# New orders of work in the attending stage of a decoder layer

## The reference

```python
x = layernorm(x + mix(x))                      # token mixing by per-head Fourier products and a running sum
q, k, v = heads(x @ W_q + b_q), heads(ctx @ W_k + b_k), heads(ctx @ W_v + b_v)     # 16 heads of 32, 77 keys
scores = where(mask == 0, -1e6, q @ k.T / sqrt(32))
x = layernorm(x + (softmax(scores) @ v) @ W_o + b_o)
x = layernorm(x + x @ quantized(kernel) + bias + (x @ a) @ b)
```

## Time and profile before

| what | us |
|---|---|
| median of 3 runs | 965.15 (964.72 to 967.47) |
| profiled execution, span | 964.6 |
| TensorE busy in it | 917.6 (95%) |
| VectorE, ScalarE, GpSimd busy | 666.7, 376.8, 337.8 |
| mean granted TensorE clock | 0.982 of full speed |
| attending stage in it | from 475.5 to the end |

### The profile page before, as it was taken

The page is one execution under the profiler, slowest core; times in us unless marked ns, Lnnn a source line. Parts: engine busy times, 40 slices in busy tenths (PEclk is TensorE's granted clock), DMA queues, the critical chain, the costliest instruction groups (busy, mean ns, idle before and its releaser), DMA issues.

```text
span 964.6 us, 14638 instructions
## 1 busy us (share of the span) xinstructions
PE 917.6 (95%) x4476; PEld 754.5 (78%) x4476; DVE 666.7 (69%) x1128; ACT 376.8 (39%) x1403; POOL 337.8 (35%) x310
## 2 busy tenths in 40 slices
PE   5898999999999999999779999999999999999987
PEld 4784888888888888888668788888888888888775
DVE  3363466665656565555667888979889798887957
ACT  3152120101010111102287566656567565666610
POOL 2000243232222232324236434444443444433733
PEclk9998999999999999999979999999999999999999
DMA  5944201221203020203423122131222203120021
GB/s 179 326 148 172 90 1 52 80 80 52 104 28 127 3 87 1 88 23 116 134 81 102 25 79 73 40 113 24 89 63 78 75 21 122 30 89 21 17 77 44
DMA packets 72346, 76.02 MB, mean 79 GB/s; under 512 B 38567, under 2 KB 40871, under 8 KB 72303
## 3 DMA queue, kind: packets, MB, share of 16 engines
q1 hardware_dynamic: 72303, 75.49, 24.4%
HBM read 52.60 MB, written 22.87 MB: 78 GB/s over the span
## 4 chain that ended last, share of the span: by engine, by line
PE 41%; DVE 4%; ACT 2%; issue 2%; POOL 2%; POOLq 0%; DVEq 0%
PE shared_ps L74 31%; PE score_ps L74 4%; PE shared_ps L1146 4%; ACT probs L1352 2%; PE shared_ps L1109 1%; PE shared_ps L1179 1%; POOL probs L1501 1%; DVE score_ps L1658 1%; DVE xT_lo L1615 0%; DVE x_and_res L1704 0%; DVE top_s L1663 0%; DVE pT_lo L1642 0%; POOL x_and_res L1516 0%; DVE y L1682 0%; DVE w_o_lo L1825 0%
## 5 line engine op out<-in xcount | busy, mean ns | idle before, releaser
L1352 ACT ACTIVATE probs<-score_ps,top_s 128x77 f32<-128x77 f32 x512 | 159.0, 359 | 36.9 <-DVE top_s L1663 36.9
L1352 ACT ACTIVATION_READ_ACCUMULATOR probs<-score_ps,top_s 128x1 f32 x512 | 122.9, 240 | 0.0
L1501 POOL TENSOR_TENSOR probs<-probs,per_total 128x616 f32<-128x616 f32 x64 | 82.7, 1309 | 65.9 <-DVE per_total L1670 65.7
L1494 POOL TENSOR_TENSOR rstd<-ve,half_power 128x1 f32<-128x1 f32 x64 | 42.4, 662 | 157.1 <-DVE ve L1693 152.5
L722 POOL TENSOR_TENSOR vals<-qs_prod 128x512 f32<-128x512 f32 x32 | 41.1, 1296 | 127.1 <-DVE qs_prod L804 127.1
L713 POOL TENSOR_TENSOR mix_rstd<-mix_ve,half_power 128x1 f32<-128x1 f32 x32 | 22.0, 688 | 175.4 <-DVE mix_ve L823 175.4
L1658 DVE COPY_PREDICATED score_ps<-hidden,masked 128x616 f32<-128x616 int32 x64 | 66.2, 1034 | 11.6 <-PE score_ps L74 11.6
L1359 ACT ACTIVATE pT_hi<-shared_ps 103x512 fp32r<-103x512 f32 (+1 forms) x96 | 54.7, 612 | 46.0 <-PE shared_ps L1146 45.5
L672 ACT ACTIVATE v_sb<-v_ps 128x512 f32<-128x512 f32 x32 | 18.9, 594 | 133.9 <-PE v_ps L74 133.9
L679 ACT ACTIVATE qT_hi<-vals 128x512 fp32r<-128x512 f32 x32 | 19.4, 631 | 122.3 <-POOL vals L722 106.2
L1642 DVE TENSOR_TENSOR pT_lo<-shared_ps,pT_hi 103x512 fp32r<-103x512 f32 (+1 forms) x96 | 64.5, 684 | 0.0
(11 more groups left out here) (218 smaller groups left out, 2660.1 us busy)
## 6 DMA issues: line engine op xcount, KB each, us to landing
x_tok<-in_x SPq DMA_DIRECT2D x8, 1024.0 KB, 5.9
x_res<-in_x SPq DMA_DIRECT2D x8, 1024.0 KB, 8.0
x_between<-mix_x SPq DMA_DIRECT2D x32, 256.0 KB, 2.0
x<-x_between SPq DMA_DIRECT2D x8, 1024.0 KB, 5.5
x_tok<-x_between SPq DMA_DIRECT2D x8, 1024.0 KB, 5.7
out<-y_out SPq DMA_DIRECT2D x32, 256.0 KB, 2.0
wqkv_sb<-in_w_qkv SPq DMA_DIRECT2D x4, 768.0 KB, 7.8
keys_split<-w_q_hi SPq DMA_DIRECT2D x8, 154.0 KB, 5.4
```

The lines of the kernel that those rows point to most:

```text
L1352: nc.scalar.activation(probs[:, t % 2, j * KEYS:(j + 1) * KEYS], score_ps[:, g, k * KEYS:(k + 1) * KEYS], ACT.Exp, bias=top[:, t % 2, j:j ...
L1494: nc.gpsimd.tensor_tensor(rstd[:, n:n + 1], ve[:, n:n + 1], half_power[:], ALU.pow).then_inc(rstd_ready, 1)
L1501: nc.gpsimd.tensor_tensor(p, p, per_total[:, t % 2, h * heads:(h + 1) * heads].unsqueeze(2) .to_broadcast([P, heads, KEYS]), ALU.mult).the ...
```

## The change

All lists of `attend` are written anew: that of the banks in all kinds of step (that of the end only in its line breaks), and those of TensorE, ScalarE, GpSimd and VectorE. The end's list of TensorE stays. No call is added or dropped. The core of the diff, with the bank orders, TensorE's full step and start step, the first part of ScalarE's full step, GpSimd's full step, the first half of VectorE's full step, and the last lines of VectorE's end:

```diff
-BANK_ORDER = ["V0", "V1", "V2", "V3", "O0", "P00", "O1", "P01", "O2", "T0", "P02", "F0", "P10", "P11", "T1",
-              "O3", "X0", "X1", "X2", "F1", "X3", "T2", "P12", "Q0", "F2", "P20", "P21", "Q1", "T3", "Q2",
-              "P22", "F3", "P30", "P31", "P32", "Q3"]
-
-
-START_ORDER = ["P00", "P01", "P02", "X0", "X1", "X2", "X3", "P10", "P11", "P12", "Q0", "P20", "P21", "Q1",
-               "P22", "Q2", "P30", "P31", "P32", "Q3"]
-CLOSING_ORDER = ["V0", "V1", "V2", "V3", "O0", "P00", "O1", "P01", "P02", "T0", "O2", "P10", "P11", "P12",
-                 "F0", "T1", "O3", "P20", "P21", "F1", "T2", "P22", "P30", "F2", "T3", "P31", "P32", "F3"]
-END_ORDER = ["V0", "V1", "V2", "V3", "O0", "O1", "O2", "T0", "O3", "T1", "F0", "T2", "F1", "T3", "F2", "F3"]
+BANK_ORDER = ["V0", "V1", "V2", "V3", "P00", "O0", "P01", "O1", "P02", "T0", "O2", "O3", "P10", "X0",
+              "F0", "P11", "T1", "X1", "X2", "P12", "X3", "F1", "Q0", "T2", "P20", "Q1", "F2", "P21",
+              "T3", "P22", "Q2", "P30", "F3", "P31", "P32", "Q3"]
+
+
+START_ORDER = ["X0", "X1", "X2", "P00", "P01", "X3", "P02", "P10", "P11", "Q0", "P12", "Q1", "P20",
+               "Q2", "P21", "P22", "Q3", "P30", "P31", "P32"]
+CLOSING_ORDER = ["V0", "V1", "V2", "V3", "O0", "P00", "O1", "T0", "P01", "P02", "O2", "F0", "P10",
+                 "T1", "P11", "P12", "O3", "F1", "T2", "P20", "P21", "P22", "F2", "T3", "P30", "P31",
+                 "P32", "F3"]
+END_ORDER = ["V0", "V1", "V2", "V3", "O0", "O1", "O2", "T0", "O3", "T1", "F0", "T2", "F1", "T3", "F2",
+             "F3"]
...
                 score(i, s, 1, 1)
+                turn_probs(i, s, 0, 0)
                 project_o(i, s, 0)
-                turn_probs(i, s, 0, 0)
+                turn_probs(i, s, 0, 1)
                 project_o(i, s, 1)
-                turn_probs(i, s, 0, 1)
+                score(i, s, 2, 0)
+                score(i, s, 2, 1)
+                turn_probs(i, s, 0, 2)
+                turn_x2(i, s, 0)
                 project_o(i, s, 2)
-                turn_x2(i, s, 0)
-                turn_probs(i, s, 0, 2)
-                score(i, s, 2, 0)
+                project_o(i, s, 3)
+                turn_probs(i, s, 1, 0)
+                turn_x1(i + 1, s, 0)
                 project_f(i, s, 0)
-                turn_probs(i, s, 1, 0)
                 turn_probs(i, s, 1, 1)
+                score(i, s, 3, 0)
                 turn_x2(i, s, 1)
-                project_o(i, s, 3)
-                score(i, s, 2, 1)
-                turn_x1(i + 1, s, 0)
                 turn_x1(i + 1, s, 1)
                 turn_x1(i + 1, s, 2)
+                score(i, s, 3, 1)
+                turn_probs(i, s, 1, 2)
+                turn_x1(i + 1, s, 3)
                 project_f(i, s, 1)
-                turn_x1(i + 1, s, 3)
+                project_q(i + 1, s, 0)
                 turn_x2(i, s, 2)
-                turn_probs(i, s, 1, 2)
-                score(i, s, 3, 0)
-                score(i, s, 3, 1)
-                project_q(i + 1, s, 0)
+                turn_probs(i, s, 2, 0)
+                project_q(i + 1, s, 1)
                 project_f(i, s, 2)
-                turn_probs(i, s, 2, 0)
                 turn_probs(i, s, 2, 1)
-                project_q(i + 1, s, 1)
                 turn_x2(i, s, 3)
+                turn_probs(i, s, 2, 2)
                 project_q(i + 1, s, 2)
-                turn_probs(i, s, 2, 2)
+                turn_probs(i, s, 3, 0)
                 project_f(i, s, 3)
-                turn_probs(i, s, 3, 0)
                 turn_probs(i, s, 3, 1)
                 turn_probs(i, s, 3, 2)
                 project_q(i + 1, s, 3)
-
 
             s = Shared(0, False, True, True)
             score(0, s, 0, 0)
             score(0, s, 0, 1)
             score(0, s, 1, 0)
             score(0, s, 1, 1)
+            turn_x1(1, s, 0)
+            turn_x1(1, s, 1)
+            turn_x1(1, s, 2)
             score(0, s, 2, 0)
             turn_probs(0, s, 0, 0)
             turn_probs(0, s, 0, 1)
+            turn_x1(1, s, 3)
             turn_probs(0, s, 0, 2)
-            turn_x1(1, s, 0)
             score(0, s, 2, 1)
-            turn_x1(1, s, 1)
+            turn_probs(0, s, 1, 0)
             score(0, s, 3, 0)
-            turn_x1(1, s, 2)
-            turn_x1(1, s, 3)
-            turn_probs(0, s, 1, 0)
             turn_probs(0, s, 1, 1)
+            project_q(1, s, 0)
+            score(0, s, 3, 1)
             turn_probs(0, s, 1, 2)
-            score(0, s, 3, 1)
-            project_q(1, s, 0)
+            project_q(1, s, 1)
             turn_probs(0, s, 2, 0)
+            project_q(1, s, 2)
             turn_probs(0, s, 2, 1)
-            project_q(1, s, 1)
             turn_probs(0, s, 2, 2)
-            project_q(1, s, 2)
+            project_q(1, s, 3)
             turn_probs(0, s, 3, 0)
             turn_probs(0, s, 3, 1)
             turn_probs(0, s, 3, 2)
-            project_q(1, s, 3)
...
                 s = Shared(i, True, True, True)
                 split_o(i - 1, s, 0)
                 exponentials(i, 0, 0)
+                exponentials(i, 0, 1)
                 split_o(i - 1, s, 1)
-                exponentials(i, 0, 1)
                 split_o(i - 1, s, 2)
                 split_o(i - 1, s, 3)
+                split_probs(i, s, 0, 0)
                 exponentials(i, 1, 0)
-                split_probs(i, s, 0, 0)
+                split_probs(i, s, 0, 1)
                 exponentials(i, 1, 1)
-                split_probs(i, s, 0, 1)
+                split_probs(i, s, 0, 2)
                 split_x2(i, s, 0)
-                split_probs(i, s, 0, 2)
+                exponentials(i, 2, 0)
+                exponentials(i, 2, 1)
                 split_probs(i, s, 1, 0)
+                split_x1(i + 1, s, 0)
                 split_probs(i, s, 1, 1)
                 split_x2(i, s, 1)
-                exponentials(i, 2, 0)
...
                 bias_residual(i - 1, 0)
+                normalize_probs(i, 0, 0)
+                normalize_probs(i, 0, 1)
                 bias_residual(i - 1, 1)
                 bias_residual(i - 1, 2)
+                root(i, s, "O0")
+                normalize_probs(i, 1, 0)
+                bias_x2(i, s, 0)
+                normalize_probs(i, 1, 1)
+                root(i, s, "O1")
                 bias_residual(i - 1, 3)
-                normalize_probs(i, 0, 0)
-                normalize_probs(i, 0, 1)
-                root(i, s, "O0")
-                bias_x2(i, s, 0)
-                root(i, s, "O1")
-                normalize_probs(i, 1, 0)
-                normalize_probs(i, 1, 1)
+                root(i, s, "O2")
                 bias_x2(i, s, 1)
-                root(i, s, "O2")
+                root(i, s, "O3")
+                normalize_probs(i, 2, 0)
+                normalize_probs(i, 2, 1)
+                root(i, s, "F0")
                 bias_x2(i, s, 2)
-                root(i, s, "F0")
-                root(i, s, "O3")
-                bias_x2(i, s, 3)
-                normalize_probs(i, 2, 0)
-                root(i, s, "F1")
-                normalize_probs(i, 2, 1)
-                root(i, s, "F2")
                 normalize_probs(i, 3, 0)
                 normalize_probs(i, 3, 1)
+                root(i, s, "F1")
+                root(i, s, "F2")
+                bias_x2(i, s, 3)
                 root(i, s, "F3")
...
                 softmax_top(i, 0, 0)
+                softmax_top(i, 0, 1)
+                invert_totals(i, 0)
                 split_o(i - 1, s, 0)
-                softmax_top(i, 0, 1)
                 split_o(i - 1, s, 1)
-                invert_totals(i, 0)
                 split_o(i - 1, s, 2)
                 split_o(i - 1, s, 3)
                 softmax_top(i, 1, 0)
+                split_probs(i, s, 0, 0)
                 softmax_top(i, 1, 1)
                 add_o(i, s, 0)
                 measure(i, s, "O0")
-                split_probs(i, s, 0, 0)
-                add_o(i, s, 1)
                 normalize_o(i, s, 0)
-                measure(i, s, "O1")
                 split_probs(i, s, 0, 1)
                 invert_totals(i, 1)
+                add_o(i, s, 1)
+                measure(i, s, "O1")
+                softmax_top(i, 2, 0)
+                split_probs(i, s, 0, 2)
+                split_x2(i, s, 0)
+                normalize_o(i, s, 1)
                 add_o(i, s, 2)
-                normalize_o(i, s, 1)
-                split_x2(i, s, 0)
+                softmax_top(i, 2, 1)
                 measure(i, s, "O2")
-                split_probs(i, s, 0, 2)
-                softmax_top(i, 2, 0)
+                add_o(i, s, 3)
+                normalize_o(i, s, 2)
+                measure(i, s, "O3")
...
             add_f(B, s, 2)
-            normalize_f(B, s, 1)
             measure(B, s, "F2")
             add_f(B, s, 3)
+            measure(B, s, "F3")
             normalize_f(B, s, 2)
-            measure(B, s, "F3")
             normalize_f(B, s, 3)
+
```

246 lines of the change are left out of this document (121 added, 125 removed).

## The result

The changed kernel takes 974.69 us (median of 4 runs, 972.22 to 977.07); the kernel before takes 965.57 (4 runs, 964.72 to 967.47). The ratio is 1.0086, with a 95% interval of 1.0066 to 1.0107: slower by some 8 us, where 958.6 was forecast. The time lies above the range of 951.5 to 968.0.

A forecast was written before the change was run, and what follows sets the result against it. Holes at the edges were taken to bound it, the middle being full of TensorE work: 965.15 - 5.0 - 1.3 + 2.5 - 2.5 - 0.2 = 958.65 us, with 8 in 10 between 951.5 and 968.

The forecast's parts named there:

- 0.5 us lost in each: Middle steps: each goes from 58.70 to 59.2 us, five steps +2.5; bounds -3 and +10.
- (b): Middle step, TensorE: T1 waits 0.65 for P10's remainder, behind add O3, normalize O2 and measure O3 on VectorE.
- The section on the port: Middle step: tile 1's mask operation on VectorE, sharing ports with GpSimd, gets in after one bias sum, ending at 651.95.
- the walk: Stepping through each engine's in-order queue with prices from the trace; it gave 58.9 for a middle step.
- (a): Middle step, TensorE: score group 2 of half 1 waits 0.7 for the second exponentials of tile 1.
- Rival A: Steps 1 to 6: mask operation waits for both bias sums, 1.4 later each, +8.4; 967.05, with the clock 976; chance 0.14.
- (c): Middle step: VectorE waits 0.75 for the root after measure O0, covered by VectorE's slack.
- 5.0 forecast: Start step: x1 turns and q projections moved earlier; step 1's score group starts at 512.9 instead of 517.90.
- 1.3 forecast: Step 1: 2.33 + 1.5 saved at project_f, 1.0 lost at V0, 1.0 charged to new waits; 1.3 us gained.
- A gain of 2.5 forecast: Step 7: three waits for probabilities, 1.8 together, go; new wait 0.9 at P20; walk 3.1, bounds 0.5 and 3.8.
- The gain of 0.5 on the last normalization: End: measure F3 ahead of normalize F2 shortens the root wait by 0.5; T3 waits 0.3 more; 0.2 gained in all.
- The chance of 0.18 on slower: Whole kernel: chance of ending slower by more than 0.3%, made up of the missed mask turn and other losses.

The follow-up runs named there:

- one_bias_later: Changed kernel with one edit: GpSimd issues bias_x2(1) behind root O3 instead of ahead of it; 969.02 us against 967.18 for the kernel before, ratio 1.0017.
- mended: New start and middle with P10/X0 copies and remainders earlier and GpSimd's sums moved, old step 7 and end; 961.96 us against 966.31 for the kernel before.
- the freed port: Changed kernel with GpSimd's sums in the full step moved to where no VectorE instruction was seen held; 965.98 us, ratio 0.9995 to the kernel before.
- the last kernels: GpSimd's clears wait for the hidden mask: on the kernel before with only the new start, 964.65 us; on new start and middle with all mends, 962.55.
- The four edits: Reorderings of GpSimd's and VectorE's step 7 lists, on the kernel before with new step 7 and end; ratios 1.0011, 1.0037, 1.0016, 1.0016.

## Why the prediction was wrong

**Where the miss lies.** By the profiles, -6.5 was forecast and +6.8 measured. Of the 13.3 between them, 7.3 are in the middle steps, 3.0 in the start, 3.5 in step 7 (1.3 of them the clock) and 0.5 in step 1; the end gives 1.2 back, which is the clock, and 0.3 is the later beginning of the stage.

**The middle steps: the step that failed.** "0.5 us lost in each" was 1.95. The mechanism was named, an instruction's length beside GpSimd was left out of it, and the sum was shaded.

(b), the wait at T1 for P10's remainder, was named, with the right bank, queue and neighbours, and sized 0.65; it measured 1.54. The term that was mis-sized is the normalization of O2 ahead of that remainder: the forecast has no price for it beside GpSimd, and it took 1.39 beside a sum, 0.55 without (shown by `one_bias_later`: 0.84 off the instruction, 0.84 off the wait). The section on the port looked at one mask operation and at no other VectorE instruction. Counted from the start of the step, TensorE came to T1 at 31.9 for 32.2 in the walk, since (a) did not occur, and T1 began at 33.5 for 32.9: of the 0.9, 0.3 is TensorE's being early and 0.6 the remainder's being late.

(a), 0.7 at score group 2 for the exponentials, did not occur. The forecast let the mask in after one bias sum, to end at 651.95; it got in at the border and ended at 650.82, and the second exponentials of tile 1 ended at 657.20 for 658.12. Rival A, the mask that misses its turn, thus failed in the middle steps, and was right in kind in step 1, where it is 2.5 us in some profiles and not 1.4 in each of six steps. That its time with the clock, 976, lies near the measured 974.69 is chance.

The sum was discounted. The waits at P00 and F2, 0.4 and 0.6 a step, were not in the list or stood under what the walk rounds. Adding waits to the busy time gave 59.8, and 59.2 was taken, nearer to a walk with shorter spacings, which came to Q3 at 56.3 of the step where the trace has 57.8. That busy time and idle time add up to a step is so by definition; what the runs show is that the busy time hardly depends on the order: 58.0 to 58.4 in every middle step at full clock, old, new and mended. Over it, waits of 0.72 a step give the 58.83 of the freed port, and 1.64 the 59.74 of the one sum. With 59.8 the forecast would have been 3 us higher, still too low.

(c), VectorE's wait for root O0, measured 0.77 for 0.75 forecast (normalization at 656.42) and was covered, as said.

**The start.** The mechanism was right, the size too large: 5.0 forecast, 2.0 in the profile of the changed kernel. With the mask operation at 1.30, and in the last kernels at 0.32, it is 3.4 to 4.5 (42.33 less 38.97 to 37.85). The term left out is that operation, the first of the stage on VectorE, beside the clears; the 0.5 to 1.0 that is left at 0.32 is unexplained.

**Step 1.** 1.3 forecast, 0.8 to 1.0 measured, with no half clock (granted clock 1.00 in its window for 0.97), as said. But the gain is the clock alone: at 1.00 the old order took 60.10 and the new one 60.92, with waits of 0.94 at V0, 0.47 at P00 and 1.44 at T1 for the one of 2.33. And the terms of the forecast, 2.33 + 1.5 - 1.0 - 1.0, make 1.8 and not 1.3.

**Step 7.** A gain of 2.5 forecast, a loss of 1.0 in the profile, of which the clock is more than all: at 1.00 it is a gain of 0.3 (49.0 for 49.36), and with the old middle ahead of it a loss of 0.2 (49.55). The forecast wait at P20 was 0.9 and measured 1.4; T2's 1.0 and O0's 0.6 were not in the walk. The four edits moved these waits and mended none of them. What bounds the step stays open: VectorE was busy for 43 to 44 us of it, and that no order of its list would do better is not shown.

**End.** T3 waited 0.3 more, as forecast. The gain of 0.5 on the last normalization came to 0.2 on its wait and nothing on the whole. Like with like, the new end costs 0.3 to 0.4: 40.7 to 40.9 against 40.3 and 40.5 where the clock stayed up, 42.4 to 42.5 against 42.0 to 42.2 where it fell. The last normalization waited 0.51 for its root where it had 0.74, because root F3 now ran beside the normalization of F2:

```profile
967.51 0.80 POOL L1494 TENSOR_TENSOR rstd<-ve,half_power 128x1 f32<-128x1 f32 x1 [1.35 <-DVE ve L1692]
```

Of the eleven roots of the end, the three beside a normalization took 0.76 to 0.80, the others 0.55. From the start of the last matmul to the end of the last normalization both kernels take 4.0 us.

**The outcome.** The loss of 9.1 (974.69 less 965.57) is the 9.8 of the middle steps, less what start and end give, with a remainder of some us that varies from execution to execution (972.22 to 977.07). The chance of 0.18 on slower was placed on the one mechanism that didn't act where it was looked for. The bounds given with the terms (+10 for the middle, 3 for start and step 1, 0.5 for step 7) reach 971.5, 3.5 over the 968 that was stated, and the lower ones 949.7, under the stated 951.5.

## What to carry to other kernels

When an order is moved, go through the VectorE instructions that the traces show held (here the mask operations, the normalizations and the one that makes the hidden mask) and ask which GpSimd instruction now lies beside them; those ahead of an item that frees a PSUM bank cost the wait their full stretch. Treat TensorE's busy time plus the waits of your list as the forecast and don't shade it by a walk. Before a difference between two profiles is read as the order's, compare the granted clock of the stretch: in this case it alone makes 1.3 to 1.6 us. A late remainder needs its copy on ScalarE early too, and an edit in one queue shows only where the next one stands: a wait removed is a gain only if the profile shows no other behind it.
